# Reordering the last attention round and the routing lead-in of a one-core transformer layer

## Time and profile before

| what | us |
|---|---|
| median of 3 runs | 843.13 (838.98 to 844.96) |
| the profiled execution: its time | 840.18 |
| its span in the trace | 838.3 |
| cross attention, linear attention, routing | start to about 450 |
| the experts | about 450 to the end |
| PE busy | 798.5 |
| DVE busy | 640.2 |
| ACT busy | 565.7 |

### The profile page before, as it was taken

How to read it: one execution, slowest core, us unless ns; L and a number is a source line. 1 busy time by engine, 2 the same in 40 slices (tenths; PEclk the granted TensorE clock), 3 DMA queues, 4 the chain that set the end, 5 groups by cost and what they waited for, 6 DMA issues and landing times.

```text
span 838.3 us, 24109 instructions
## 1 busy us (share of the span) xinstructions
PE 798.5 (95%) x9278; PEld 696.6 (83%) x9278; DVE 640.2 (76%) x1033; ACT 565.7 (67%) x879; POOL 282.0 (34%) x190
## 2 busy tenths in 40 slices
PE   6999999999999999997897999999999999999993
PEld 5566588998999999996886888998889888898883
DVE  4445543756757575674788999999999999999992
ACT  2645456554656665472256899999899999988971
POOL 1333384020220202010001345555555555555541
PEclk9999999999999999999699999999999999999997
DMA  9999920000000000004962445544555445554452
GB/s 339 415 417 415 384 80 2 2 16 16 15 28 3 28 3 28 18 13 183 426 260 70 120 132 149 148 133 125 140 154 137 132 126 144 156 136 128 127 144 42
DMA packets 31771, 115.92 MB, mean 138 GB/s; under 512 B 4465, under 2 KB 11570, under 8 KB 26578
## 3 DMA queue, kind: packets, MB, share of 16 engines
q1 hardware_dynamic: 22834, 100.17, 33.4%
q0 software_dynamic: 8864, 14.69, 8.2%
HBM read 105.27 MB, written 9.57 MB: 137 GB/s over the span
## 4 chain that ended last, share of the span: by engine, by line
PE 88%; DVE 4%; issue 2%; ACT 1%; DMA 1%; SPq 0%; POOL 0%; POOLq 0%; DVEq 0%; ACTq 0%
PE ps L536 23%; PE ps L538 22%; PE ps L537 22%; PE ps L925 4%; PE ps L741 3%; PE ps L712 2%; PE ps L582 2%; PE ps L635 2%; PE ps L594 2%; PE ps L616 1%; PE ps L888 1%; PE ps L613 1%; PE ps L572 1%; PE ps L807 1%; DMA bor<-in_bo 1%
## 5 line engine op out<-in xcount | busy, mean ns | idle before, releaser
L1570 DVE TENSOR_TENSOR w_lo<-w,w_hi 128x1024 fp32r<-128x1024 f32 x156 | 187.4, 1224 | 1.1 <-issue 1.1
L522 POOL DMA_INDIRECT out_x<-y_sb,slot_row x39 | 123.7, 3173 | 117.9 <-ACT y_sb L1171 117.9
L1139 ACT ACTIVATE w_hi<-w 128x1024 fp32r x156 | 161.2, 1060 | 2.4 <-DVE tile_e L1614 2.4
L536 PE MATMUL ps<-w_hi,xh 128*128 128x512 f32 x312 | 125.8, 403 | 1.4 <-DVE xl L1663 1.3
L538 PE MATMUL ps<-w_hi,xl 128*128 128x512 f32 x312 | 122.0, 391 | 0.0
L537 PE MATMUL ps<-w_lo,xh 128*128 128x512 f32 x312 | 121.6, 390 | 0.0
L536 PE MATMUL ps<-xT_hi,wa_hi 128*128 128x256 f32 x384 | 109.4, 285 | 2.1 <-issue 1.0
L537 PE MATMUL ps<-xT_lo,wa_hi 128*128 128x256 f32 x384 | 107.9, 281 | 0.0
L538 PE MATMUL ps<-xT_hi,wa_lo 128*128 128x256 f32 x384 | 107.8, 281 | 0.0
L1150 ACT ACTIVATE w_hi<-w_sb 128x1024 fp32r<-128x1024 f32 x78 | 82.6, 1063 | 27.7 <-DMA w_sb<-in_w 15.2
L510 POOL DMA_INDIRECT xs_sb<-xn_d,slot_row x39 | 67.3, 1726 | 98.8 <-PE ps L888 78.4
(11 more groups left out here) (219 smaller groups left out, 1767.3 us busy)
## 6 DMA issues: line engine op xcount, KB each, us to landing
w_sb<-in_w SPq DMA_DIRECT2D x78, 512.0 KB, 4.5
ctx_t<-in_ctxT SPq DMA_DIRECT2D x16, 1028.0 KB, 9.0
ctx_n<-in_ctxN SPq DMA_DIRECT2D x16, 1024.0 KB
w<-in_w SPq DMA_DIRECT2D x8, 2048.0 KB, 14.8
stage<-in_w_a SPq DMA_DIRECT2D x16, 256.0 KB, 8.7
x_all<-in_x SPq DMA_DIRECT2D x4, 512.0 KB, 9.3
out_x<-x_all POOLq DMA_DIRECT2D x8, 256.0 KB, 3.2
xn_d<-xn_first POOLq DMA_DIRECT2D x6, 256.0 KB, 2.8
```

The lines of the kernel that those rows point to most:

```text
L522: pool.indirect_dma_start(out, bass.IndirectOffsetOnAxis(slot_row[:, t:t + 1], 0), y_sb[:, :], None, compute_op=ALU.add).then_inc(f_st, 16)
L536: pe.matmul(dst, l_hi, r_hi, start=first, stop=False)
L1139: act.activation(w_hi[:, c, :].rearrange("p (c n) -> p c n", c=DC), w13[:, bass.ds(e, 1), c % 2, :, c // 2 * 512:(c // 2 + 1) * 512].rearr ...
L1570: dve.tensor_tensor(w_lo[:, c, :].rearrange("p (c n) -> p c n", c=DC), w13[:, bass.ds(e, 1), c % 2, :, c // 2 * 512:(c // 2 + 1) * 512].re ...
```

## The change

Only orders, banks and waits change; no arithmetic does.

- **Round 7 on PE**: S7,1 follows S7,0 at once, then V7,1 second half, D, G3. DVE's `masks` stays at the head of its drain. ACT's `den_ev(7)` moves ahead of the tanh of G3.
- **Banks**: P6 and P7 go to bank 2 (`out_bank`), so that N7 no longer waits for `x2(6)`. The logits of part 0 go to bank 3, those of part 1 to bank 6.
- **Drain on PE**: P6,0, N7,0, P6,1, N7,1, T0, T1, P7,0, L0, P7,1, T2, L1, T3, L2, T4, L3, T5, L4, L5, T6, L6, T7, L7.
- **Drain on ACT**: each `gated_hi(7)` stands behind one of the evictions of T0 and T1; `g_sqrt(6)` stands behind that of T2.
- **Drain on DVE**: `g_lns(5)` moves from ahead of the reciprocals to between `gated(7,1)` and `gated_lo(7,1)`, `x2(6)` from the middle of them to behind `gated(7,0)`, and `top_two(0)` from ahead of `x2(7)` to between `g_stats(7)` and `g_lns(7)`.

```diff
-    LOGIT_BANK = (2, 3, 4)
+    LOGIT_BANK = (3, 6, 4)
+
+    def out_bank(r):
+        return 2 if r >= NT // 2 - 2 else 6
...
         def a_nums(r, s):
             wait(pe, a_norm, 2 * r + s + 1)
-            wait(pe, a_x2, r)
+            wait(pe, a_x2, r if r < NR - 1 else r - 1)
+            if r == NR - 1:
+                wait(pe, a_de, 2 * r + 2)
...
         def a_proj(r, u, s, cs=range(FC)):
-            wait(pe, a_o, 8 * r + 8)
+            if r < NR - 1:
+                wait(pe, a_o, 8 * r + 8)
+            if r == NR - 2:
+                wait(pe, a_vu, 4 * (NR - 1) + 3)
+            if r == NR - 1:
+                wait(pe, a_x2, r)
...
-                m = mm3(ps[:, 6, s * D:(s + 1) * D], goh[:, c, rows], gol[:, u, c, rows], w_out_hi[:, c, :], w_out_lo[:, c, :],
+                m = mm3(ps[:, out_bank(r), s * D:(s + 1) * D], goh[:, c, rows], gol[:, u, c, rows], w_out_hi[:, c, :], w_out_lo[:, c, :],
...
                 a_scores(r, 0)
+                a_scores(r, 1)
                 a_values(r, 1, range(1, 2))
+                a_dens(r)
                 a_gates(r, range(3, 4))
-                a_scores(r, 1)
                 return
...
         def g_logits(r):
             wait(pe, g_xT, r + 1)
+            if part_of(2 * r):
+                wait(pe, a_o, 8 * NR)
...
         def drain(r, u):
-            a_proj(r - 1, 1 - u, 0, range(0, FC // 2))
-            a_dens(r)
-            a_proj(r - 1, 1 - u, 0, range(FC // 2, FC))
+            a_proj(r - 1, 1 - u, 0)
+            a_nums(r, 0)
             a_proj(r - 1, 1 - u, 1)
+            a_nums(r, 1)
             g_trs(0)
             g_trs(1)
+            a_proj(r, u, 0)
             g_logits(0)
-            a_nums(r, 0)
+            a_proj(r, u, 1)
             g_trs(2)
             g_logits(1)
-            a_nums(r, 1)
             g_trs(3)
             g_logits(2)
-            a_proj(r, u, 0)
-            a_proj(r, u, 1)
+            g_trs(4)
             g_logits(3)
-            g_trs(4)
             g_trs(5)
             g_logits(4)
+            g_logits(5)
             g_trs(6)
-            g_logits(5)
             g_logits(6)
...
             if r == NR - 1:
+                den_ev(r)
                 gates(r, u, range(3, 4))
...
         def drain(r, u):
-            den_ev(r)
-            for k in range(3):
-                g_xT_ev(k)
+            g_xT_ev(0)
             gated_hi(r, u, 0)
+            g_xT_ev(1)
             gated_hi(r, u, 1)
+            g_xT_ev(2)
+            g_sqrt(r - 1)
             g_xT_ev(3)
-            g_sqrt(r - 1)
...
         def gated(r, u, s):
             wait(dve, a_num, 2 * r + s + 1)
+            if r == NR - 1:
+                wait(dve, a_gtu, 4 * NR)
...
         def drain(r, u):
             masks(r)
-            g_lns(r - 2)
             recip(r, 0)
             recip(r, 1)
-            x2(r - 1)
             norm_att(r, 0)
             recip(r, 2)
             recip(r, 3)
             norm_att(r, 1)
             gated(r, u, 0)
+            x2(r - 1)
             gated_lo(r, u, 0)
             gated(r, u, 1)
+            g_lns(r - 2)
             gated_lo(r, u, 1)
             g_stats(r - 1)
-            top_two(0)
             g_lns(r - 1)
             x2(r)
             g_stats(r)
+            top_two(0)
             g_lns(r)
```

More of the change, by code:

```diff
@@ L1393, in x2 @@
             wait(dve, a_y, r + 1)
-            dve.tensor_tensor(rows, ps[:, 6, :], rows, ALU.add).then_inc(a_x2, 1)
+            dve.tensor_tensor(rows, ps[:, out_bank(r), :], rows, ALU.add).then_inc(a_x2, 1)
         def g_stats(r):
```

## The result

| kernel | median, us | range | runs |
|---|---|---|---|
| before | 845.08 | 838.98 to 846.63 | 8 |
| changed | 849.07 | 843.85 to 851.86 | 8 |

The ratio is 1.0061, 95% interval 1.0037 to 1.0086: 3 to 7 us slower. I had forecast 842 and no change, in a range that ended at 847. The profiled execution of the changed kernel took 850.07, with a span of 848.2, 9.9 more than the profiled one of before. Not all of that is the change: 3.6 lie ahead of S7,0 (383.03 against 379.45), where the order is the same, and 1.8 behind ACT's first expert weights.

The account below looks back on a forecast made before the run. Bound: a chain crossing engines in round 7 and the lead-in to the ranks, not PE work. Shifts -4.7, -0.2, +0.8, +2.5, +1.5 sum to -0.1: 840.1 us profiled, 842 as median; range 835 to 847.

Parts of the forecast that it names:

- Part 1: Round 7's two scores side by side on PE: first instruction stall stays, a second of 2.5 us follows S7,1.
- The rival without a second gap: At the scores: no second stall behind S7,1, everything 2.5 us earlier, 837.6 us; chance 0.17.
- Part 2: Masks, D and reciprocals: 4.7 us gained, 3.0 by D and 1.6 by `x2(6)`; expert transfers 4 us later but hidden.
- Part 3: P6, N7, T0: `goh` queued on ACT behind T0's eviction gives back 3.5 us; P7,0 at 405.1 instead of 409.93.
- part 4: PE clock under P7: half clock for 5.9 us into P7, P7,1 ends at 414.3 against 418.3, gain 4.0.
- Part 5: DVE's tail: `x2(7)` 2.7 us behind P7,1, then 10.3 to `top_two(2)`, at 427.3 against 427.36; the gain goes.
- the slow rival: Half clock from before P7,0 until L5, PE takes over from DVE: + 6 us, 846.2; chance 0.12.
- The frame: Whole forecast: work after `top_two(2)` on DVE is unchanged, so its shift is the shift of the end.

Follow-up runs that it names:

- e4: Changed kernel with P6,0 (24 long matmuls) moved from the drain to between S7,0 and S7,1; ratio 1.0029 to the kernel before.
- e12: e6 with P7,0 moved ahead of T3 and L2 and its six fillers spread over the tail; ratio 0.9960 to the kernel before.
- e2: Changed kernel with ACT's `gated_hi(7,0)` moved ahead of the evictions of T0 and T1; ratio 0.9985 to the kernel before.
- e13: Changed kernel with only its six fillers spread over the tail on PE, none ahead of the ranks; ratio 1.0004 to the kernel before.
- e5: Changed kernel without the six filler matmuls ahead of the ranks; ratio 1.0022 to the kernel before.
- e3: Changed kernel with ACT's `g_sqrt(6)` moved ahead of the eviction of T2; ratio 1.0028 to the kernel before.
- e7: Changed kernel with T0 to T3 and L0 to L2 back ahead of P7, and ACT's order with them; ratio 1.0041 to the kernel before.
- e6: e7 with P6,0 between S7,0 and S7,1 and `top_two(0)` ahead of `g_lns(6)`; ratio 0.9986 to the kernel before.
- e1: Changed kernel with S7,1, D and `den_ev(7)` back at their old places; median 845.7, ratio 1.0027 to the kernel before.
- e9: e6 with its six fillers spread over the tail on PE; ratio 0.9994 to the kernel before.
- e10: e8 with `top_two(0)` moved behind `g_lns(7)`; ratio 0.9998 to the kernel before.
- e8: Changed kernel with the edits of e2, e3 and e5 together; ratio 0.9976 to the kernel before.

## Why the prediction was wrong

**Part 1 was right.** The first gap stayed where it was, the second came: V7,1 at +7.57, forecast +7.5. The rival without a second gap is out. So is, for these bursts, what the Trainium skill's page "Runtime: NRT & Kernel Launch" says in the section "Instruction fetch mechanics", that a crossing is mostly hidden. e4 and the packets bear out instruction supply.

**Part 2 had the right steps and missed the clock.** V took 2.7 us instead of 1.4, because the clock fell 4.2 us behind S7,0, behind the first gap: D at +10.3 for +8.9. The forecast looked for low clock at P7 only. By N7,1 the delay was 1.8. The late transfers were rightly found hidden in the changed kernel; in e12 they are not.

**Part 3 and part 4 were right in mechanism.** `goh` waits behind T0's eviction, and e2 puts its price at 2.6, where I had 3.5. P7 starts at half clock and rises in it; it took 8.1 for my 9.2. Their errors nearly cancel: from N7,1 to P7,0, with its stall and T0, T1 at half clock, 6.3 for 5.4 (+0.8), and P7 -1.1. That, with 0.3 less at `x2(7)`'s queue, is why `x2(7)` came only 1.2 late: luck, not accuracy.

**Part 5 is what failed.** Its queue was right: `x2(7)` came 2.4 behind P7,1, forecast 2.7. Its cover stops at L5: "four pairs of T and L and one L need some 6.5 us behind 414.3 at full clock". They took 6.6, and L5 did come in time. But the sum has no term for T6, L6, T7 and L7 behind it; it takes them for hidden under DVE and gives no reason. They ran at half clock and took 7.0 (the slow rival has 5.0 for them), and L7 was 1.44 late. 10.3 became 11.5, 1.2 more. e13, at full clock, has the 10.3.

**The frame failed too:** "what follows it is the same work in the same order. Its shift is my forecast of the shift of the end". The work between `top_two(2)` and the ranks is the same, but six fillers stand on PE ahead of the ranks. Before, they ended with DVE; at half clock and behind a late L7 they hold the ranks until +55.3. That is 5.9 us instead of 3.7, a further 2.2. e5 takes 1.5 of it out (4.3), and e13 takes out as much and the late L7 with it.

Together: +2.4 at `top_two(2)`, of which 1.2 were there at `x2(7)` and 1.2 are L7's, and +2.2 behind it are the 4.6 us; the measured ratio makes 5. Spreading the fillers, which also held the clock, took 3.0 of it back within the tail (17.4 less e13's 14.4). My slow rival had this mechanism, with PE taking over from DVE and + 6 us, but set its start before P7. I gave it a chance of 0.12, as I took the rise within P7 for a sign that the low level would end there. I did not ask what PE would do in the 13.6 us between P7,1 and the ranks' turn, where before there were 7.5.

What stays open: the marks are those of one execution each, and where the clock falls differs from one to the next in the stretch ahead of P7 (e3 has 10 us low at once, e7 6.8 and 10.2). Why e7 has more of it than e6 I did not settle. Nor is the scores' share of the median settled (e1), nor how much of the fillers' 1.5 is their place and how much their half clock; and why the clock falls in the tail at all was not tested, only that spread fillers keep it up (e9, e12, e13).

## What to carry to other kernels

When work is gathered behind the last dense matmuls, ask what PE's clock will be there, and cost the small matmuls at the rate that the trace shows for half clock. A filler has a price in the critical chain if the chain's next matmul stands behind it; spread in waits that exist anyway it costs little, and it can hold the clock (e13 against the changed kernel: 3.7 us at the ranks). A queue on ACT is cheap to mend: one line moved in e2 gave 3 us at the ranks.

## What the runs showed that was not expected

- The burst S7,0, 256 instructions within 1.3 us, is followed by a gap of 2.0 to 2.7 us in every kernel here. Where S7,1 follows at once, a second gap of 2.2 to 2.5 us stands behind it; where 24 long matmuls stand between (e4), there is none.
- Where the fillers stand counts with how long they take: twelve such matmuls in a row took 5.47 us at half clock, all of it ahead of the ranks; in e13, four of the spread ones took 1.03 at full clock, in a wait that was there anyway.
- In the changed kernel's tail PE was busy for 12.33 of 13.70 us, with no wait above 0.69, and the clock was 0.51 all the same. The tail had 13.7 us of half clock in e1, e2, e3, e4, e5, e7 and e10 as well, and 20 in e8.
